# Attention into the first 512 nodes of a graph network computed from a dense count matrix, beside the gathers for the other nodes

## The chip, the cores and the metric

One core of a Trainium2 chip runs the whole program in one launch. The metric is device microseconds (us) of one execution, from the first instruction to the last, as the median of several.

## The reference

A pre-norm graph network of four layers over N = 3125 nodes with D = 128 features and 103125 directed edges (50000 in both directions and one loop per node), sorted by destination. Three layers sum or average neighbours; the fourth, which matters here, is attention along the edges:

```
Q, K, V = x@Wq+bq, x@Wk+bk, x@Wv+bv            # 8 heads of 16 features
score = exp(clip(sum(K[src]*Q[dst], -1) / 4, -5, 5))
wV = segment_sum(V[src] * score, dst);  z = segment_sum(score, dst)
h = layer_norm(x + wV / (z + 0.001), gamma1, beta1)
out = x_in + h + relu(layer_norm(h, gamma2, beta2) @ Wo + bo)
```

## The kernel before

Three parts follow one another. **build_counts** (0 to 338 us) makes from the edge list a dense matrix `counts`: 25 tiles of 128 sources in the partitions, 3136 destinations along a row, bf16; an entry is the number of edges between the two. **dense_layers** (338 to 1125 us) runs seven passes over the 25 node tiles; `z_bank` collects products of `y_parts` (a float32 value as three bf16 parts) with `counts`. Pass 6 also makes queries, keys and values and stores them: `keys_values` (1 KB a node) and `query_parts`. SP issues each tile's loads and stores in program order on its queue (`s_in`, `residual`, `self_term` and so on, function `sync_passes` and its helpers).

**attention** (1125 us to the end) goes by edges. A step is 512 edges, four chunks of 128; six steps are a group, with 34 groups and NS = 202 steps. POOL gathers with four indirect DMAs a step the source rows of `keys_values` into a ring of six steps (L1474). ACT makes the one-hot of each edge's destination (square L1509, relu L1516); PE spreads the queries to the edges by it (L1576, `aq_bank`); DVE multiplies by the gathered keys (`prod`, L1711), makes the one-hot the other way (`pick`, L1714), sums over a head (L1717), multiplies the values of the step before by their weights (`msg`, L1722) and clips the scores (L1727); ACT takes the exponentials (L1534, L1537); PE aggregates a group's six steps into 128 destination rows (`acc_bank`, L1592), two steps behind. Each group then ends with `sum_up` (ACT, L1548), `attended`, `first_norm`, `second_norm`, `result` on DVE, two `rstd` on ACT with a table load ahead of each Ln and Exp (L1525, L1526), a transposition and a projection on PE. All engines run a loop of two groups per turn, written out step by step, with the first group and the last three outside the loop. The order in an engine is that of the code; semaphores alone tie the engines together.

Of the kernel before, what the change touches and what calls it, by code (L numbers as in the profile page):

```python
# [41 lines left out]
NG = -(-E // GE)  # L42
NS = -(-E // (GC * P))
LASTBASE = N - P
QW = 42
# [8 lines left out]
PEELED = 5  # L54
AHEAD = 4
# [94 lines left out]
def over_tiles(chain, step, lag):  # L150


    for dt in range(PEELED):
        before = chain.steps
        step(Num(dt))

    def body(k):
        for j in range(TURN):
            step(Num(PEELED + j, k, TURN))

    chain.loop((NT - PEELED) // TURN, (chain.steps - before) * TURN, body)
    for dt in range(NT, NT + lag):
        step(Num(dt))


def over_tiles_ending(chain, step, lag):


    for dt in range(PEELED):
        before = chain.steps  # L170
        step(Num(dt))

    def body(k):
        for j in range(TURN):
            step(Num(PEELED + j, k, TURN))

    chain.loop((NT - PEELED) // TURN - 1, (chain.steps - before) * TURN, body)
    for dt in range(NT - TURN, NT + lag):
        step(Num(dt))

# [25 lines left out]
def program(nc, t):  # L206
    with ExitStack() as ctx:
# [9 lines left out]
        v.query_parts = dram("query_parts", (NP, YW), BF16)  # L217
        v.rel_rows = dram("group_rel_rows", (NC * P,), BF16)
# [66 lines left out]
def build_counts(nc, t, v, counts):  # L285
# [8 lines left out]
    with ExitStack() as ctx:  # L294
# [39 lines left out]
        base_row = sb("group_first", [1, LEAD + NG + 4], I32)  # L334
        query_row = sb("query_first", [1, QN * (NG + 3)], I32)
        gap = sb("gap", [1, NG])
        gap_flag = sb("gap_flag", [1, 2])
# [20 lines left out]
        def _(sp):  # L358
# [19 lines left out]
            sp.dma_start(v.first_index[:, :], t["src_cols"][:, 0:(GS - 1) * GC]).then_inc(first_in, 16)  # L378
# [63 lines left out]
        def _(dve):  # L442
# [15 lines left out]
            chain.step(nc.vector.tensor_scalar(v.bases[:, :], base_row[:, :], float(LASTBASE), None, ALU.min))  # L458
# [5 lines left out]
            chain.step(nc.vector.tensor_scalar(gap_flag[:, 1:2], v.bases[:, LEAD + NG - 1:LEAD + NG], float(LASTBASE), None, ALU.is_lt))  # L464
            chain.step(nc.vector.tensor_tensor(gap_flag[:, 0:1], gap_flag[:, 0:1], gap_flag[:, 1:2], ALU.max))
            dve.wait_ge(rel_ready, 2)
# [146 lines left out]
def dense_layers(nc, t, v, counts, by_edge=False):  # L613
# [6 lines left out]
    with ExitStack() as ctx:  # L620
# [11 lines left out]
        bq = y3[0][:, 7, 0:2 * D].bitcast(F32)  # L632
        bias = [sb("bias_even", [P, 2 * D]), sb("bias_odd", [P, D])]
# [33 lines left out]
        bias_summed, part_ready, qkv_ready = sem("bias_summed"), sem("part_ready"), sem("qkv_ready")  # L667
        z_ld, z_zeroed = (sems("z_ld"), sem("z_zeroed")) if by_edge else (None, None)
# [21 lines left out]
        def sync_passes(sp, passes):  # L690
# [64 lines left out]

            if by_edge:
                sp.wait_ge(z_zeroed, passes[0] + 1)
# [6 lines left out]
            for p in passes:  # L764
                if p == 6:
                    sp.wait_ge(z_ready, NT * 5)
                    sp.dma_start(wq, t["L3_gnn_Wq"]).then_inc(w_q, 16)
                    sp.dma_start(bq, t["L3_gnn_bq"].partition_broadcast(P)).then_inc(w_q, 16)

# [3 lines left out]
                def step(dt):  # L773
# [11 lines left out]
                    stage(lambda d: store_queries(p, d), dt, PEELED - 1)  # L785

                over_tiles_ending(sp_chain, step, PEELED - 1 if p == 6 else min(LAG[p][3] + 2, PEELED - 1))
            if 6 not in passes:
                return
            for sem_, n in ((s_st, nth(ALL, 6, Num(NT - 1))), (x_st, nth(X_OUT, 6, Num(NT - 1))), (h_st, Num(NT - 1)),  # L790
                            (q_st, Num(NT - 1))):
                for back in range(len(sem_)):
                    (n - back).landed(sp, sem_, held)

        def pool_passes(pool, passes):
# [48 lines left out]

            for p in passes:
                if p:
                    weights_landed(pool, p)
                if p == 2:
# [3 lines left out]
                def step(dt):  # L852
# [5 lines left out]
                    stage(lambda d: sum_norm(p, d), dt, 0)  # L858

                over_tiles(chain, step, LAG[p][3] + 1)  # L860

        def tensor_passes(pe, passes):
# [3 lines left out]
            def transpose(p, dt):  # L866
                n = nth(ALL, p, dt)
                (n + 1).count(pe, h_ready)
                (n - 1).count(pe, hT_ready)
                nc.tensor.transpose(t_bank[n.slot()][:, 0:P], h[:, n.slot(), :], v.ident[:, :]).then_inc(t_done, 1)  # L870

            def products(p, dt):
# [12 lines left out]
                if p == 6:  # L885
                    ins = nc.tensor.matmul(out_[:, 2 * D:3 * D], hT[:, n.slot(), :], wq, start=True, stop=True)
                ins.then_inc(d_done, 1)
# [80 lines left out]
            for p in passes:  # L968
# [20 lines left out]
                over_tiles(chain, step, TURNED[p])  # L989

        def scalar_passes(act, passes):
# [24 lines left out]
            def query_part(p, dt):  # L1016

                if p == 6:
# [3 lines left out]
                    else:  # L1022
                        (dt - 2).landed(act, q_st)
                    nc.scalar.activation(q_part[:, dt.slot(), 0:D], qkv[:, dt.slot(), 2 * D:3 * D], ACT.Copy,
                                         scale=float(DH) ** -0.5).then_inc(part_ready, 1)

# [56 lines left out]
            for p in passes:  # L1083
                def step(dt):
# [12 lines left out]
                    if p == 6:  # L1097
                        stage(lambda d: query_part(p, d), dt, last + 2)
                    if not norm:
                        stage(lambda d: next_h(p, d), dt, norm)  # L1100

                over_tiles(chain, step, LAG[p][3] + 2 * (p == 6))

        def vector_passes(dve, passes):
# [128 lines left out]
            for p in passes:  # L1233
# [22 lines left out]
                over_tiles(chain, step, LAG[p][3] + 1 + 2 * (p == 6))  # L1256
# [18 lines left out]
def attention(nc, t, v, counts):  # L1275
# [7 lines left out]
    QUERIES_AHEAD = 2  # L1283
    QB = 3
    THIRD, THIRD_SHIFT = 171, 9
    MR = 6
    PAIR = 2 * GS
    WIDE = GC * P
    BN, MV, LOG, RSTD = slice(0, 6), slice(6, 8), 8, 9
    with ExitStack() as ctx:  # L1290
# [14 lines left out]
        out_sum, res = room.take("out_sum", [P, D]), room.take("res", [P, 2, D])  # L1305
        src_cols = sb("a_src", [P, NC], I32)
# [18 lines left out]
        q_bank, acc_bank = ps("aq_bank", QB), ps("acc_bank", 2)  # L1325
        (small_bank,), (place_bank,) = ps("at_bank", 1), ps("place_bank", 1)
        t_bank, c_bank = small_bank[:, 0:P], small_bank[:, P:P + D]
        places, upper = place_bank[:, 0:P], place_bank[:, P:P + 1]
        (weight_bank,) = ps("weight_bank", 1)
        weights = weight_bank[:, 0:2 * GC * H].rearrange("p (n c h) -> p n c h", n=2, c=GC)  # L1330
# [13 lines left out]
        held = sem("a_held")  # L1344
        block = ctx.enter_context(nc.Block())
# [12 lines left out]

        def by_power(g):
# [3 lines left out]
        def over_steps(step, chain=None, per_turn=0):  # L1363
# [8 lines left out]
            turns = NG // 2 - 2  # L1372
# [4 lines left out]
        def tail(step):  # L1377
            for i in range(PAIR * (NG // 2 - 1), PAIR * (NG // 2) + GS + 3):
# [3 lines left out]
        def _(sp):  # L1382
            sp.dma_start(src_cols[:, :], t["src_cols"]).then_inc(src_ld, 16)
            sp.dma_start(rel_cols[:, :], v.rel_cols).then_inc(cols_ld, 16)
            sp.dma_start(first_wide[:, :], t["group_first"].partition_broadcast(P)).then_inc(cols_ld, 16)
# [12 lines left out]
            def load_wide(g):  # L1398
# [3 lines left out]
                sp.dma_start(rel_wide[:, g.slot(), :], v.rel_rows[bass.ds(g.value(GE), GE)].partition_broadcast(P)).then_inc(  # L1402
# [10 lines left out]
            def load_h(g, base):  # L1413
                (g - 1).count(sp, h1_ready, held)
                sp.dma_start(h_in[:, g.slot(), :], v.h[bass.ds(base, P), :]).then_inc(h_ld[g.slot()], 16)

            def load_x(g, base):
                (g - 1).count(sp, res_ready, held)
                sp.dma_start(x_in[:, g.slot(), :], v.x[2][bass.ds(base, P), :]).then_inc(x_ld[g.slot()], 16)

            def store(g, base):
                (g + 1).count(sp, res_ready, held)
                sp.wait_ge(out_st, (g + 1).value(16))
                sp.sem_inc(held, 1)
                sp.dma_start(t["out"][bass.ds(base, P), :], res[:, g.slot(), :]).then_inc(out_st, 16)

            def turn(g, both, i):
                regs, query_regs = both
                if group(g + 1):
                    load_wide(g + 1)  # L1430
                    load_queries(g + 1, query_regs[i * QN:i * QN + QN])
                if group(g):
# [11 lines left out]
            load_queries(Num(0), first_bases)  # L1444
            sp.dma_start(wo[:, :], t["L3_gnn_Wo"]).then_inc(w_ld, 16)
# [8 lines left out]
            with sp.Fori(0, NG // 2 - 2) as k:  # L1454
# [3 lines left out]
            for p in range(NG // 2 - 1, NG // 2 + 1):  # L1458
                regs = bases(p)
                for i in range(2):  # L1460
                    turn(Num(2 * p + i), regs, i)
            sp.wait_ge(out_st, NG * 16 + 16)
# [759 lines left out]
```

## Time and profile before

| | us |
|---|---|
| median of three executions | 2166.93 (2166.40 to 2169.04) |
| profiled execution | 2167.79, its span 2166.1 |
| attention, of the span | 1125 to 2166 |
| busy over the span | PE 1557.6, DVE 1399.9, POOL 1173.9, ACT 1094.2 |
| mean granted TensorE clock | 0.696 of full speed |

Busy shares are means over parts with other limits; the attention part is read by itself, from 150 us stretches and from the chain of work that ended last. A full speed of 1.00 of the granted clock is 2.4 GHz, and 0.50 is 1.2 GHz.

### The profile page before, as it was taken

The page shows a single profiled execution, that of the slowest core. Times are in us where ns is not written, and L with a number is a line of the kernel's source. Part 1 is how long each engine was busy: PE and PEld are TensorE (multiplying, and loading weights), DVE is VectorE, ACT ScalarE, POOL GpSimd, SP SyncE. Part 2 cuts the span into 40 slices and gives each one's busy share as a digit, 9 for nine tenths or more (in the row PEclk, how much of TensorE's full clock was granted, in tenths as well). Part 3 has the DMA queues.
Part 4 walks back from the last instruction along what each step waited for, and adds up shares of the span by engine and source line. Part 5 has one row for each costly group of instructions (what it writes and reads, how often), then busy time and mean ns, then how long its engine had stood idle before and what let it go on. Part 6 is the DMA issues. An engine that isn't in the chain of part 4 may idle for free. (4 is left out here: it accounts for less than half of the span.)

```text
span 2166.1 us, 41707 instructions
## 1 busy us (share of the span) xinstructions
PE 1557.6 (72%) x7805; PEld 1038.9 (48%) x7805; DVE 1399.9 (65%) x3771; ACT 1094.2 (51%) x2721; POOL 1173.9 (54%) x1478
## 2 busy tenths in 40 slices
PE   2677776899998999999965556556655566555564
PEld 1232333465555666666644445445444455444453
DVE  7999996545655643335656666666666666666665
ACT  6788885433553422222225555555555555555552
POOL 6645554323543411011127777777777777777774
PEclk9555557999999999999985555555555555555555
DMA  3000001101111110111345444444444444444442
GB/s 149 0 0 0 0 0 49 46 28 44 53 52 53 55 38 29 32 29 58 102 143 157 140 132 142 146 145 144 127 142 145 145 138 133 142 145 144 144 128 63
DMA packets 158830, 192.74 MB, mean 89 GB/s; under 512 B 39725, under 2 KB 126894, under 8 KB 158510
## 3 DMA queue, kind: packets, MB, share of 16 engines
q0 software_dynamic: 38784, 105.96, 16.8%
q1 hardware_dynamic: 119982, 86.09, 12.9%
q8 instruction: 20, 0.33, 0.1%
q14 instruction: 44, 0.36, 0.1%
HBM read 163.23 MB, written 25.04 MB: 87 GB/s over the span
## 5 line engine op out<-in xcount | busy, mean ns | idle before, releaser
L1474 POOL DMA_INDIRECT counts<-keys_values,a_index x788 | 747.0, 948 | 240.1 <-issue 172.5
L895 PE MATMUL z_bank<-y_parts,counts 128*128 128x384 bf16 (+1 forms) x3658 | 641.9, 327 | 1.2 <-DVE y_parts L1231 0.6
L1592 PE MATMUL acc_bank<-counts 128*128 128x136 f32 x1616 | 426.6, 443 | 197.2 <-DVE counts L1722 180.9
L1592 PEld LDWEIGHTS acc_bank<-counts 128*128 128x128 f32 x1616 | 364.8, 321 | 247.5 <-DVE counts L1722 226.0
L895 PEld LDWEIGHTS z_bank<-y_parts,counts 128*128 (+1 forms) x3658 | 358.4, 98 | 228.8 <-issue 5.5
L1711 DVE TENSOR_TENSOR counts<-aq_bank,counts 128x512 f32<-128x512 f32 x202 | 139.6, 691 | 315.0 <-DMA counts<-keys_values,a_index 303.6
L1576 PE MATMUL aq_bank<-counts 126*128 126x128 bf16 x808 | 118.2, 299 | 238.9 <-DVE counts L1711 221.1
L1534 ACT ACTIVATE weight_bank<-a_clipped 128x32 f32<-128x32 f32 x202 | 40.0, 198 | 457.3 <-DVE a_clipped L1727 457.1
L428 POOL TENSOR_TENSOR key_low_build<-iota_b_build,src_cols_build 128x768 bf16<-128x768 bf16 x102 | 155.2, 1522 | 149.8 <-DVE flat_build L506 130.4
L1576 PEld LDWEIGHTS aq_bank<-counts 126*128 126x128 bf16 x808 | 73.7, 129 | 287.0 <-issue 263.1
L1122 DVE TENSOR_REDUCE z_sum<-z_bank 128x128 f32<-128x384 f32 x150 | 83.6, 557 | 165.2 <-PE z_bank L895 160.8
L524 DVE TENSOR_TENSOR counts<-share_build,counts 128x275 f32 x408 | 157.3, 440 | 9.9 <-PE share_build L602 5.8
L602 PE MATMUL share_build<-flat_build,src_tile_build 128*128 128x275 bf16 x408 | 108.3, 422 | 75.4 <-ACT src_tile_build L568 40.6
L1509 ACT ACTIVATE a_apart<-counts,a_query_lane 128x512 bf16<-128x512 bf16 x204 | 144.1, 706 | 12.5 <-DMA counts<-group_rel_rows 12.5
L506 DVE TENSOR_TENSOR flat_build<-iota_wide_build,src_cols_build 128x2200 bf16<-128x2200 bf16 x102 | 144.2, 1415 | 2.4
L1516 ACT ACTIVATE counts<-a_apart,a_one 128x512 bf16<-128x512 bf16 x204 | 144.1, 706 | 0.2
L602 PE MATMUL share_build<-flat_build,left_build 128*128 128x275 bf16 x408 | 108.4, 423 | 42.8 <-ACT left_build L568 39.8
L1722 DVE TENSOR_TENSOR counts<-counts,weight_bank 128x512 f32<-128x512 f32 x202 | 136.7, 677 | 0.8 <-ACT weight_bank L1534 0.8
L1717 DVE TENSOR_REDUCE a_score<-counts 128x32 f32<-128x512 f32 x202 | 137.0, 678 | 0.0
L1714 DVE TENSOR_TENSOR counts<-a_rel,place_bank 128x512 f32<-128x512 f32 x202 | 136.7, 677 | 0.0
L1004 ACT ACTIVATE hT<-t_bank 128x128 f32<-128x128 f32 x175 | 48.5, 277 | 170.8 <-PE t_bank L870 166.1
L884 PE MATMUL d_bank<-weights,hT 128*128 128x256 f32 x350 | 114.4, 409 | 18.1 <-ACT hT L1004 17.8
(183 smaller groups left out, 2132.3 us busy)
## 6 DMA issues: line engine op xcount, KB each, us to landing
counts<-group_rel_rows SPq DMA_DIRECT2D x34, 768.0 KB, 5.3
counts<-keys_values,a_index POOLq DMA_INDIRECT x788, 2.7
self_term<-s_out SPq DMA_DIRECT2D x150, 64.0 KB, 1.6
s_in<-self_term SPq DMA_DIRECT2D x150, 64.0 KB, 1.8
residual<-x_in SPq DMA_DIRECT2D x75, 64.0 KB, 1.6
counts<-counts SPq DMA_DIRECT2D x2, 1792.0 KB, 11.4
counts<-query_parts SPq DMA_DIRECT2D x102, 31.5 KB
x_in<-in_x SPq DMA_DIRECT2D x50, 64.0 KB, 1.8
```

Of the source, the lines that this page charges most:

```text
L428: nc.gpsimd.tensor_tensor(square[:, g.slot(), :, :].rearrange("p (h c) n -> p h c n", h=2)[:, :, 0:BY_POOL, :], place.unsqueeze(1).unsquee ...
L506: nc.vector.tensor_tensor(right[:, g.slot(), :, :, :], iota_wide[:, :, :].unsqueeze(1).to_broadcast([P, 2, KW, 4]), keys.unsqueeze(2).to_b ...
L524: nc.vector.tensor_tensor(window, share[GB * j + i][:, 0:KW].rearrange("p (t w) -> p t w", w=WP), window, ALU.add).then_inc(column_sums, 1)
L602: ins = nc.tensor.matmul(share[j * GB + i][:, 0:KW], left[j][:, i % 2 * GB + c, :], right[:, j, i % 2, :, c], start=c % 2 == 0, stop=c % 2 ...
L895: return nc.tensor.matmul(bank(p, dt)[:, 0:width], counts[:, bass.ds(dt.value(P) + source * NA, P)], y3[(p - 1) % 2][:, source, 0:width], ...
L1474: nc.gpsimd.indirect_dma_start(rows_kv[:, j, c, :], None, v.kv, bass.IndirectOffsetOnAxis(column, 0)).then_inc(gathered[j], 16)
L1509: return chain.start(nc.scalar.activation(apart[:, s.slot(), :], rel_wide[:, g.slot(), j * GC * P:(j + 1) * GC * P], ACT.Square, bias=quer ...
L1516: nc.scalar.activation(node_of_edge[:, g.slot(), j * GC * P:(j + 1) * GC * P], apart[:, s.slot(), :], ACT.Relu, bias=one[:, :], scale=-1.0 ...
L1576: ins = nc.tensor.matmul(q_bank[s.slot(QB)][:, c * P:c * P + P], node_of_edge[0:PARTS * QW, g.slot(), (j * GC + c) * P:(j * GC + c) * P + ...
L1592: ins = nc.tensor.matmul(acc_bank[ga.slot()][:, 0:TW], pick[:, s2.slot(MR), c, :], msg[:, s2.slot(MR), c, :], start=j == 2 and c == 0, sto ...
L1711: nc.vector.tensor_tensor(prod[:, :].rearrange("p (c d) -> p c d", c=GC), q_bank[s.slot(QB)][:, :].rearrange("p (c d) -> p c d", c=GC), ro ...
L1717: nc.vector.tensor_reduce(score[:, s.slot(), :], prod[:, :].rearrange("p (n d) -> p n d", d=DH), AX.X, ALU.add).then_inc(sum_done, 1)
```

## The change

The first 31 steps of the attention (15872 edges, all with a destination below 512) are left out: 171 steps in 29 groups remain, and edge, column and query indices are shifted by `SKIP`. The nodes 0 to 511 (DN = 512, four tiles) get their attention from the dense counts in 200 units, one for each of the 25 source tiles and 8 heads, spread over the six steps of groups 0 to 24 as 2, 2, 1, 1, 1, 1. A unit is: a bf16 score product on PE (three parts of keys by three of queries, stacked along the contraction), `below` (Relu) and `power` (Exp) on ACT, `weighted` on DVE (the larger of the exponential and e^-5, times the counts), and a float32 product with the values on PE, which adds all sources in two `value_bank`s.

```
+HEADS = ((0, 1), (2, 3), (4,), (5,), (6,), (7,))
+def below(s, g, h):
+    (u + 1).count(act, scored)
+    nc.scalar.activation(room_below[:, u.slot(), :], score_bank[:, :], ACT.Relu, bias=five[:, :], scale=-1.0).then_inc(limited, 1)
+def power(s, g, h):
+    (u - (PR - 1)).count(act, valued)
+    nc.scalar.activation(weighted[:, u.slot(PR), :], room_below[:, u.slot(), :], ACT.Exp, bias=five[:, :], scale=-1.0).then_inc(powered, 1)
+def score(g, h):
+    u.count(pe, limited)
+    nc.tensor.matmul(score_bank[:, :], key_stack[:, g.slot(), h, :], query_stack[:, h, :], start=True, stop=True).then_inc(scored, 1)
+def value(g, h):
+    (u + 1).count(pe, weighed)
+    nc.tensor.matmul(value_bank[h // 4][:, :], values[:, g.slot() * 2 + h // 4, h % 4 * P:h % 4 * P + P], weighted[:, u.slot(PR), :], ...)
 # DVE, a step, after the clip
+for gw, h in heads(s1, g, j - 1):
+    (u + 1).count(dve, powered)
+    nc.vector.scalar_tensor_tensor(weighted[:, u.slot(PR), :], weighted[:, u.slot(PR), :], LOWEST, tile_counts[:, gw.slot(), :],
+                                   ALU.max, ALU.mult).then_inc(weighed, 1)
 # PE, a step
 spread(s + QUERIES_AHEAD, ...)
+for _, h in now[0:1]: score(g, h)
+for gv, h in heads(s2, g, j - 2): value(gv, h)
 ... acc_bank products of step s - 2 ...
+for _, h in now[1:2]: score(g, h)
```

To make room in PSUM, `aq_bank` has two buffers, not three (`QUERIES_AHEAD` 1, not 2), `acc_bank` one, not two, and the step weights move into `place_bank`, so that `pick` waits for the weights of the step before:

```
-    QUERIES_AHEAD = 2
-    QB = 3
+    QUERIES_AHEAD = 1
+    QB = 2
+                    s.count(dve, weigh_done)
                     nc.vector.tensor_tensor(pick[:, s.slot(MR), :, :], ...
```

The four dense tiles are finished by the same chain as a group, at steps 155, 157, 161 and 163, between the last groups. DVE takes `result`, `second_norm`, `first_norm`, `attended` after the `weighted` units.

Keys and queries must also stand with features in the partitions. Pass 6 gets one more product per tile, `kT`, and in its first four tiles `qT`, two (four) activations on ACT, three (six) POOL instructions that split them in bf16 parts, and a store; nine tiles stand ahead of its loop, not five:

```
+ins = nc.tensor.matmul(out_[:, 3 * D:4 * D], wk_turned, hT[:, n.slot(), :], start=True, stop=True)
+ins = nc.tensor.matmul(t_bank[n.slot()][:, P:2 * P], wq_turned, hT[:, n.slot(), :], start=True, stop=True)
+sp.dma_start(v.kt[...], kT_part[:, dt.slot(), :, :]).then_inc(kT_st[dt.slot()], 16)
```

The first 512 columns of all count tiles are stored to memory at the start of pass 4 (25 x 128 rows of 1 KB, 3200 KB), and read back by tiles in the attention, with the turned keys and the values, five DMAs a group (`load_tile`); `load_stack` reads the turned queries once, eight DMAs of 128 KB:

```
+if p == 4 and not by_edge:
+    sp.dma_start(v.dense_counts.rearrange("(t p) n -> p t n", p=P), counts[...][:, :, 0:DN]).then_inc(dense_st, 16)
```

On PE the first steps of a loop turn stand as follows before (`aq_bank` is the spread of the queries, `acc_bank` the aggregation, `at_bank` transposition and projection of an earlier group):

```order
L1576 MATMUL aq_bank<-counts 128x128 x4
L102 REGISTER_ALU
L1592 MATMUL acc_bank<-counts 128x136 x4
L102 ISA
L1605 MATMUL at_bank<-ident,counts 128x128
L102 REGISTER_ALU x2
L1576 MATMUL aq_bank<-counts 128x128 x4
L1592 MATMUL acc_bank<-counts 128x136 x4
L102 REGISTER_ALU
L1600 MATMUL acc_bank<-counts 128x136
L1611 MATMUL at_bank<-a_wo,counts 128x128
```

and now, the same place (`score_bank` and `value_bank` are a unit's two products):

```order
L1848 MATMUL aq_bank<-counts 128x128 x4
L1500 ISA
L108 ISA
L1873 MATMUL score_bank<-counts 128x512
L108 REGISTER_ALU
L1861 MATMUL value_bank<-counts 128x512
L108 REGISTER_ALU
L1892 MATMUL acc_bank<-counts 128x136 x4
L108 REGISTER_ALU
L1873 MATMUL score_bank<-counts 128x512
L108 ISA
L1915 MATMUL at_bank<-ident,counts 128x128
```

Between the spread and the aggregation of a step stand a score and a value product, and a second score behind it; the score waits there for ACT's `below` of the unit before.

On SP, from the end of pass 3 to the first loads of pass 4, the issues are now (before, L813 is not there and all else is the same):

```order
L759 DMA residual<-x_in 128x128
L771 DMA self_term<-s_out 128x128 x3
L813 DMA dense_counts<-counts 128x25x512
L731 DMA s_in<-self_term 128x128
L721 DMA weights<-in_L_gnn_W_neigh 128x128
L721 DMA weights<-in_L_gnn_W_self 128x128
L723 DMA bias_odd<-in_L_gnn_b_self 128x128
L731 DMA s_in<-self_term 128x128 x3
```

The store of the counts is queued ahead of the `s_in` loads and the weights of the next pass.

## Rows read from the trace of the kernel before

**Rows 1.** The page's costliest groups: the attention's instructions (count, busy, mean ns, idle)
```profile
L1474 POOL DMA_INDIRECT counts<-keys_values,a_index x788 | 747.0, 948 | 240.1 <-issue 172.5
L1711 DVE TENSOR_TENSOR counts<-aq_bank,counts 128x512 f32<-128x512 f32 x202 | 139.6, 691 | 315.0 <-DMA counts<-keys_values,a_index 303.6
...
L1516 ACT ACTIVATE counts<-a_apart,a_one 128x512 bf16<-128x512 bf16 x204 | 144.1, 706 | 0.2
```
**Rows 2.** Chain that ended last, 1614 to 1634 us (start, us, what)
```profile
1616.62 2.73 DMA counts<-keys_values,a_index
...
1620.38 0.94 POOL counts L1474
...
1621.62 2.70 DMA counts<-keys_values,a_index
```
**Rows 3.** Windows: busy us (instructions) of each engine, granted clock, DMA share, GB/s
```profile
core 0: us, PE busy (x) PEld busy (x) DVE busy (x) ACT busy (x) POOL busy (x), PEclk, DMA share, GB/s
55.00:330.00 275.00, 198.07 (x748) 82.64 (x747) 266.27 (x471) 230.33 (x375) 145.37 (x96) 0.51 0.00 0
...
1905.00:2055.00 150.00, 88.18 (x395) 72.59 (x395) 99.85 (x255) 82.37 (x200) 113.43 (x121) 0.52 0.47 144
1045.00:1100.00 55.00, 55.00 (x344) 36.81 (x343) 36.52 (x125) 12.69 (x35) 8.58 (x22) 1.00 0.33 103
```
**Rows 4.** Timeline of PE in the attention, 1612 to 1624 us (start, us, operation, idle before)
```profile
1612.69 0.60 PE L1576 MATMUL aq_bank<-counts 126*128 126x128 bf16 x4 [0.72 <-DVE counts L1711]
1614.47 2.18 PE L1592 MATMUL acc_bank<-counts 128*128 128x136 f32 x8 [1.18 <-DVE counts L1722]
...
1621.86 0.49 PE L1576 MATMUL aq_bank<-counts 126*128 126x128 bf16 x4
1622.19 1.15 PE L1592 MATMUL acc_bank<-counts 128*128 128x136 f32 x8
```
**Rows 5.** The same view near the end, two steps' aggregation at once
```profile
2144.37 4.01 PE L1592 MATMUL acc_bank<-counts 128*128 128x136 f32 x16 [4.25 <-DVE counts L1722]
```
**Rows 6.** Timeline, a gather that begins while a DVE addition runs
```profile
1301.90 0.29 DVE L1656 TENSOR_TENSOR counts<-counts 128x128 f32<-128x128 f32 x1
1301.95 1.07 POOL L1474 DMA_INDIRECT counts<-keys_values,a_index  x1 [0.30 <-ACT a_index L1501]
```
**Rows 7.** Timeline, 1601 to 1612 us, a second such pair on POOL and DVE
```profile
1602.70 0.29 DVE L1656 TENSOR_TENSOR counts<-counts 128x128 f32<-128x128 f32 x1
1602.82 0.99 POOL L1474 DMA_INDIRECT counts<-keys_values,a_index  x1 [0.30 <-issue]
```
**Rows 8.** Timeline, start of pass 4: a load and its use
```profile
770.20 0.34 SPq L703 DMA_DIRECT2D s_in<-self_term  x1
...
774.97 0.35 DVE L1128 SCALAR_TENSOR_TENSOR layer_out<-z_sum,inv_count,s_in 128x128 f32<-128x128 f32 x1
```
**Rows 9.** The page's DMA issues (count, KB each, median us to landing)
```profile
s_in<-self_term SPq DMA_DIRECT2D x150, 64.0 KB, 1.8
counts<-counts SPq DMA_DIRECT2D x2, 1792.0 KB, 11.4
```
**Rows 10.** Tile view of `first_index`, its 10 KB load issued behind `group_rel_cols` (448 KB)
```profile
L378 SPq DMA_DIRECT2D first_index<-in_src_cols x1: 1792/1792/1792, 20.5 to 20.5; - x1
...
DMA to landing us min/median/max: 2.7/3.7/9.2
```
**Rows 11.** Timeline of PE, pass 6
```profile
1053.56 0.38 PE L886 MATMUL d_bank<-y_parts,hT 128*128 128x128 f32 x2
1053.78 3.09 PE L895 MATMUL z_bank<-y_parts,counts 128*128 128x384 bf16 x18
```
**Rows 12.** Timeline of ACT, start of the attention
```profile
1134.52 0.72 ACT L1509 ACTIVATE a_apart<-counts,a_query_lane 128x512 bf16<-128x512 bf16 x1 [12.51 <-DMA counts<-group_rel_rows]
```
**Rows 13.** Timeline, the end: the last step's first DVE instruction
```profile
2141.84 0.69 DVE L1711 TENSOR_TENSOR counts<-aq_bank,counts 128x512 f32<-128x512 f32 x1 [3.34 <-DMA counts<-keys_values,a_index]
```

More of the change, by code:

```diff
@@ L54 @@
 PEELED = 5
+PEELED_LAST = 9
 AHEAD = 4
@@ L147, in loop, with over_tiles @@
         self.steps = start + per_turn * turns
-def over_tiles(chain, step, lag):
-    for dt in range(PEELED):
+def over_tiles(chain, step, lag, peeled=PEELED):
+    for dt in range(peeled):
         before = chain.steps
@@ L158, in body, with over_tiles_ending @@
         for j in range(TURN):
-            step(Num(PEELED + j, k, TURN))
-    chain.loop((NT - PEELED) // TURN, (chain.steps - before) * TURN, body)
+            step(Num(peeled + j, k, TURN))
+    chain.loop((NT - peeled) // TURN, (chain.steps - before) * TURN, body)
     for dt in range(NT, NT + lag):
         step(Num(dt))
-def over_tiles_ending(chain, step, lag):
-    for dt in range(PEELED):
+def over_tiles_ending(chain, step, lag, peeled=PEELED):
+    for dt in range(peeled):
         before = chain.steps
@@ L1357, in group, with tile, unit, tile_landed @@
             return g.k is not None or 0 <= g.c < NG
+        def tile(g):
+            return g.k is not None or 0 <= g.c < NT
+        def unit(g, h):
+            return Num(g.c * H + h, g.k, 2 * H)
+        def tile_landed(engine, g):
+            turn = (g.c // 2 + 1) * 80
+            engine.wait_ge(tile_ld[g.slot()], turn if g.k is None else g.k * 80 + turn)
+        def heads(s, g, j):
+            if j < 0:
+                g, j = g - 1, j + GS
+            return [(g, h) for h in HEADS[j]] if tile(g) else []
+        starts = sorted([(GS * g + GS + 3 * (g < NG - 1), "group", g) for g in range(NG)] + [(at, "tile", i) for i, at in enumerate(TILE_AT)])
+        place_of = {item[1:]: n for n, item in enumerate(starts)}
+        def nth_out(g):
+            return g if g.k is not None or g.c < NT else Num(place_of["group", g.c])
+        def nth_tile(i):
+            return Num(place_of["tile", i])
+        def tiles_at(s, lag):
+            return [i for i, at in enumerate(TILE_AT) if s.k is None and s.c - at == lag]
+        def tile_bank(i):
+            return value_bank[i // 2][:, i % 2 * 2 * P:i % 2 * 2 * P + 2 * P]
         def by_power(g):
@@ L1424, in store @@
+            def store(o, base):
+                (o + 1).count(sp, res_ready, held)
+                sp.wait_ge(out_st, (o + 1).value(16))
                 sp.sem_inc(held, 1)
[L1425 removed]
+                sp.dma_start(t["out"][bass.ds(base, P), :], res[:, o.slot(), :]).then_inc(out_st, 16)
             def turn(g, both, i):
@@ L1583, in step @@
                 s2 = s - 2
+                now = heads(s, g, j)
+                for _, h in now[0:1]:
+                    score(g, h)
+                for gv, h in heads(s2, g, j - 2):
+                    value(gv, h)
                 if sub(s2):
```

440 lines of the change are left out of this document (346 added, 94 removed).

## The prediction

> **What bounds the kernel now.** I read the page's costliest groups first, then the chain of waits, then the windows, and timelines at the places the change touches. The groups show that POOL's gathers cost 948 ns each and that POOL stood 240.1/788 = 0.305 us before each, almost all of it issue; DVE's `prod` stood 315.0 us, of which 303.6 waited for gathered rows [rows 1]. A step of four gathers is thus 4 x (0.948 + 0.305) = 5.01 us. The chain says the same: it runs from a gather's landing over DVE to the next gather and its landing, and the landings begin 5.00 us apart [rows 2]. So the attention is bound by the rate at which POOL issues gathers, and a group of six steps takes 30.06 us. In it the other engines have room: by the window from 1905 us, PE is busy 88.18/150 x 30.06 = 17.7 us, DVE 20.0, ACT 16.5 [rows 3]. PE does this at a granted clock of 0.52, its lower level of 1.2 GHz; in pass 6 it is busy without a gap at 1.00 [rows 3].
>
> **The change part by part.**
>
> *Steps left out.* 31 x 5.01 = 155.3 us less, as long as POOL stays the bound. All below asks whether it does.
>
> *The units beside the gathers.* Groups 0 to 24 take eight units each. ACT gets two 128x512 activations per unit, 16 x 0.706 = 11.3 us [rows 1], so 27.8 of 30.06. DVE gets one 128x512 operation, 8 x 0.69 = 5.5 us [rows 1], so 25.5 of 30.06. Both fit, ACT with 2.2 us left. The work of PE depends on its clock. Two steps' aggregation took 4.01 us, one 2.18 [rows 4, 5]: a further step costs 1.83 us, a 136-column float32 product 0.458, a 512-column one 0.458 x 512/136 = 1.72. The score has 512 bf16 columns, as many as a step's spread, which took 0.49 to 0.60 [rows 4]. Eight units are 17.7 to 18.6 us at the lower level. Six aggregations overlap with what follows by 2.18 - 1.83 = 0.35 each, so the old 17.7 is 15.6 start to start, and the sum 33.3 to 34.2: more than 30.06. At the upper level an aggregation took 1.15, not 2.18 [rows 4], and the sum is 17.6 to 18.0. That aggregation at the upper level came after 6 us in which PE was nearly never idle. I therefore expect that a group that runs over at 1.2 GHz leaves PE without gaps, that its clock rises, and that the six steps of gathers in the ring cover the lag: cost 0, bounds 0 and 25 x 4.1 = 103 us (rival A).
>
> *Waits added.* `pick` waits for the weights of the step before; behind it on DVE stand the sum, `msg`, the clip and the units. The weights are ACT's third instruction of a step that began with that clip, and DVE waits 303.6/202 = 1.5 us a step for rows in any case [rows 1]: 0. With one `acc_bank` the first aggregation of a group waits for `sum_up`, now first in ACT's step; the spread of the next step is queued behind it: below 1 us a group, and covered like the rest: 0. Each score waits for `below` of the unit before; the second score of a step stands behind a value product and an aggregation, over 1.8 us, in which ACT is long done (otherwise rival B).
>
> *Gathers that start under a `weighted`.* `weighted` reads two SBUF tiles. In the trace a gather is longer when a DVE addition of two SBUF tiles is in flight at its start: with 0.24 us of the addition left it took 1.07, with 0.17 left 0.99 [rows 6, 7], against the mean of 0.948: the length grows by what is left beyond some 0.12 us. With `msg` or `prod`, which read PSUM, I saw no such growth. If gathers start at any moment of the 1.25 us, a 0.65 us operation adds (0.65 - 0.12)^2/(2 x 1.25) = 0.11 us, and 200 add 22. The same formula for the 0.29 us operations, seven a group in 34 groups, gives 2.8 us; the excess over the mean that the lengthened gathers (28 of 783 in the loop) have together is about 1.9. So 22 x 1.9/2.8 = 15; I take +14, bounds 0 and 35 (0.65^2/(2 x 1.25) x 200, without the 0.12).
> The Trainium skill speaks against the change here: "SBUF — State Buffer", section "SBUF: two separate sides", says that GpSimd and a DVE operation with two SBUF inputs take one port pair in turn, each for its whole instruction. The rows agree only in part, as DVE's additions kept their 0.29 us under a gather in flight. By the rule every unit could push a gather by its full length; that is rival P.
>
> *Pass 4.* The store of 3200 KB (3.28 MB) now stands ahead of the `s_in` load that was issued at 770.20 and used at 774.97 [rows 8]. In pass 6 the DMA engines moved 103 GB/s at a share of 0.33 [rows 3], so at most 312 GB/s, and the store takes at least 10.5 us; 1792 KB took 11.4 to land [rows 9], which would make 20. A 10 KB load behind one of 448 KB took 9.2 us to land [rows 10], so loads wait for what is queued ahead. Issue at 770.2, 10.5 for the store and 1.8 for the load [rows 9] give 782.5, less 774.97: 7.5 late, and some 1.5 at a lower clock after the gap. +9, bounds 0 (the load is not held up) and 17.
> The Trainium skill, "DMA: Bandwidth & Descriptors", section "Two DMAs through the same engine are not ordered", lets the descriptors of one queue start in order and overlap; by that the load would come somewhat under the full 10.5 us later, which stays inside these bounds.
>
> *Pass 6.* PE is busy all the time, and a 128x128 float32 product holds up the next by 0.22 us [rows 11]: 29 x 0.22 = +6.4, at most 29 x 0.38 = 11 by its busy time. ACT and POOL are busy 23% and 16% of the window there [rows 3], so their parts hide, but for the last tile, whose split and store end the pass: +1.5 (0 to 4).
>
> *Start of the attention.* 13 DMAs now stand ahead of the second group's destinations (768 KB, on SP's queue); ACT waited 12.51 us for the first ones [rows 12], and these do not move. Then ACT has six steps' one-hots to make, before it needs the second. The 1.5 MB take about 5 us at 312 GB/s, partly hidden: +3 (0 to 7).
>
> *End.* Behind the last gather all is done as before [rows 13]; four more tile finishes stand among the last groups, with eight `rstd` of some 3 us that ACT has time for, since no units are left after step 150. +2 (0 to 9).
>
> Sum: 2167.8 (the profiled execution) - 155.3 + 14 + 9 + 6.4 + 1.5 + 3 + 2 = 2048.4. The median of the runs is 0.9 below the profiled execution: 2047.5, so **2047**.
>
> **Rivals.**
> *A. PE stays at 1.2 GHz and is the bound.* For it: in build_counts PE was busy 198/275 = 72% of the time at 0.51 [rows 3], so much work alone does not raise the clock. Against it: nothing there is without gaps for long, and here the overrun itself closes the gaps. At the lower level in all 25 groups: 25 x (33.3 - 30.06) = 81, to 2128, with the larger score 2150; in half of them 2088.
> *P. The port holds in full.* Each of 200 units delays POOL by its 0.65 us: 130 in place of 14, 2163, no change that could be told. Against it: a growth of at most 0.12 us is what the trace shows.
> *B. Slower: exposed turns on PE's queue.* Place: the score that waits for `below` with values, aggregation and spread queued behind it. If ACT, at 27.8 of 30.06, is late, each such wait shows a score and an activation, 0.5 + 0.7 = 1.2 us. At the lower clock two such waits a group would make 33.3 + 2.4 = 35.7, beyond the 34.9 (30.06 + 120/25) from which the change loses. With four in eight it is 38.1: 2047 + 25 x 8.0 = 2247. For it: all engines are in order and hang on each other within a step. Against: a stalled PE lags, and the ring of six steps and ACT's table of one-hots a group ahead give it slack.
> *That the change does not do what it says:* the edge path by DMA accumulation is taken if edge 15871 ends at node 512 or above; with 33 edges a node it ends near 481. Left out.
>
> **How the numbers follow.** Forecast 0.72; its own range, from the bounds of the port (0 to 35), pass 4 (0 to 17), the other edges and a part of the low clock, is 2024 to 2076. Better than 2024: 0.05. A 0.13, half of it under 2108. P 0.04, B 0.06. So 2024 to 2108 holds about 8 in 10. About 0.2%, some 4 us, is what a measurement here tells from no change; only P falls near it. Faster 0.91, same 0.02, slower 0.07.
>
> **What would show it.** POOL's gathers still 1.25 us apart through the groups with units, with `prod` waiting for the rows; mean gather 0.95 to 1.05 us; PE's granted clock in these groups above 0.52 and near 0.5 after step 150; ACT near 27.8 us a group. At the start of pass 4, a stall of 5 to 12 us behind the store; pass 6 longer by 6 to 11. The prediction is wrong if a group takes over 31.5 us, with POOL waiting for a free slot in the ring (DVE or PE late), or if gathers average over 1.1 us.

## The result, and the profile after

The changed kernel takes 2057.89 us, median of four executions (2054.04 to 2060.99), against 2167.0: a ratio of 0.9494 (95% interval 0.9475 to 0.9513). It is faster by 109 us where 120 were forecast. Its profiled execution took 2059.49 us, with a span of 2057.3. Where the difference lies between the two profiled executions:

| stretch | before | after | change | forecast |
|---|---|---|---|---|
| start to first gather | 1125.93 | 1145.81 | +19.9 | 9 + 6.4 + 1.5 = +16.9 |
| first gather to last | 1011.7 | 878.5 | -133.2 | -155.3 + 14 + 3 = -138.3 |
| last gather to the end | 28.5 | 33.1 | +4.6 | +2 |

The page's groups show that the bound is the same one as in [rows 1]: POOL's gathers, still some 0.31 us apart, with DVE's `prod` waiting for what they fetch. The mean gather went from 948 to 974 ns. PE stood 212.4/200 = 1.06 us for `below` ahead of each score.

```profile
L1695 POOL DMA_INDIRECT counts<-keys_values,a_index x664 | 646.4, 974 | 207.4 <-issue 168.6
...
L1873 PE MATMUL score_bank<-counts 128*128 128x512 bf16 x200 | 85.4, 427 | 221.4 <-ACT counts L1748 212.4
...
L2031 DVE TENSOR_TENSOR counts<-aq_bank,counts 128x512 f32<-128x512 f32 x171 | 118.1, 690 | 139.4 <-DMA counts<-keys_values,a_index 124.7
...
L1755 ACT ACTIVATE counts<-counts,a_five 128x512 f32<-128x512 f32 x200 | 142.4, 712 | 2.4
```

The windows (columns as in [rows 3]) of the groups with units and of those behind them: the granted clock is 0.88 where the units are, with PE busy 68% of the time, and 0.64 after them. Before, it was 0.52 with PE busy 59%.

```profile
1175.00:1925.00 750.00, 513.37 (x2530) 346.96 (x2531) 605.32 (x1433) 636.66 (x1372) 570.30 (x585) 0.88 0.52 151
1925.00:2020.00 95.00, 56.65 (x285) 48.23 (x283) 80.52 (x243) 80.53 (x173) 72.15 (x76) 0.64 0.47 137
```

PE's timeline in a group with units shows both levels. A score takes 0.39 us and a value product 0.86 (start to the next start) at the upper one, 0.61 and 1.70 at the lower one. It fell after two waits of 2.08 and 2.46 us in a row, and was back after the 3.4 us of unbroken work from 1615.14 to 1618.52.

```profile
1608.05 0.39 PE L1873 MATMUL score_bank<-counts 128*128 128x512 bf16 x1 [1.70 <-ACT counts L1748]
1608.27 1.02 PE L1861 MATMUL value_bank<-counts 128*128 128x512 f32 x2
1609.13 1.09 PE L1892 MATMUL acc_bank<-counts 128*128 128x136 f32 x8
1612.31 0.38 PE L1848 MATMUL aq_bank<-counts 126*128 126x128 bf16 x4 [2.08 <-DVE counts L2031]
1615.14 0.61 PE L1873 MATMUL score_bank<-counts 128*128 128x512 bf16 x1 [2.46 <-ACT counts L1748]
1615.55 1.91 PE L1861 MATMUL value_bank<-counts 128*128 128x512 f32 x2
1617.25 1.43 PE L1892 MATMUL acc_bank<-counts 128*128 128x136 f32 x8
1618.52 0.39 PE L1848 MATMUL aq_bank<-counts 126*128 126x128 bf16 x4
```

The start of pass 4, which answers to [rows 8]: behind the store, the `s_in` load is issued at 767.84 and used at 779.00, after a wait of 6.90 us; PE stood 6.0 us and ran at the lower clock for some 4 us (granted 0.50 from 780 to 784 us).

```profile
767.23 0.43 SPq L813 DMA_DIRECT2D dense_counts<-counts  x1
767.84 5.13 SPq L731 DMA_DIRECT2D s_in<-self_term  x1
...
779.00 0.35 DVE L1239 SCALAR_TENSOR_TENSOR layer_out<-z_sum,inv_count,s_in 128x128 f32<-128x128 f32 x1 [6.90 <-DMA s_in<-self_term]
...
779.81 0.48 PE L949 MATMUL t_bank<-ident,h 128*128 128x128 f32 x1 [6.01 <-ACT h L1164]
```

At the start of the attention one wait was handed on through three engines: ACT waits 9.97 us for the second group's destinations, queued on SP behind the tile and the turned queries; the weights of step 0 stand behind it on ACT; DVE's `pick` waits for them (the wait that the change adds); and POOL gets no free slot for 5.30 us.

```profile
1170.36 0.72 ACT L1730 ACTIVATE a_apart<-counts,a_query_lane 128x512 bf16<-128x512 bf16 x1 [9.97 <-DMA counts<-group_rel_rows]
...
1170.99 0.18 ACT L1778 ACTIVATE place_bank<-a_clipped 128x32 f32<-128x32 f32 x1
...
1171.20 0.69 DVE L2035 TENSOR_TENSOR counts<-a_rel,place_bank 128x512 f32<-128x512 f32 x1 [5.98 <-ACT place_bank L1778]
...
1176.67 0.94 POOL L1695 DMA_INDIRECT counts<-keys_values,a_index  x1 [5.30 <-DVE counts L2031]
```

Gathers that start under a `weighted`, as in [rows 6, 7]: the pair of units below began at 1478.78, its second operation about 0.60 later; the gather began 0.07 us into that and took 1.44.

```profile
1478.78 1.28 DVE L2053 SCALAR_TENSOR_TENSOR counts<-counts 128x512 f32<-128x512 f32 x2
...
1479.45 1.44 POOL L1695 DMA_INDIRECT counts<-keys_values,a_index  x1 [0.30 <-ACT a_index L1722]
```

### The profile page after: what moved, and what is told of

It is laid out like the page before. It is cut to its first block and busy times, and to the rows that moved or that the text cites. A ratio compares the mean times of both kernels' runs of the same rounds, so it can differ in the third digit from the quotient of the medians.

```text
span 2057.3 us, 42761 instructions
## 1 busy us (share of the span) xinstructions
PE 1559.0 (76%) x8084; PEld 965.3 (47%) x8084; DVE 1440.0 (70%) x3795; ACT 1293.3 (63%) x3022; POOL 1113.4 (54%) x1442
## 5 line engine op out<-in xcount | busy, mean ns | idle before, releaser
L1695 POOL DMA_INDIRECT counts<-keys_values,a_index x664 | 646.4, 974 | 207.4 <-issue 168.6
L1892 PEld LDWEIGHTS acc_bank<-counts 128*128 128x128 f32 x1368 | 233.0, 236 | 113.0 <-issue 91.7
L1873 PE MATMUL score_bank<-counts 128*128 128x512 bf16 x200 | 85.4, 427 | 221.4 <-ACT counts L1748 212.4
L1892 PE MATMUL acc_bank<-counts 128*128 128x136 f32 x1368 | 237.7, 328 | 18.7 <-ACT counts L1767 12.4
L1861 PE MATMUL value_bank<-counts 128*128 128x512 f32 x400 | 228.8, 678 | 2.3 <-DVE counts L2053 2.3
L2031 DVE TENSOR_TENSOR counts<-aq_bank,counts 128x512 f32<-128x512 f32 x171 | 118.1, 690 | 139.4 <-DMA counts<-keys_values,a_index 124.7
L540 DVE TENSOR_TENSOR counts<-share_build,counts 128x275 f32 x408 | 155.3, 439 | 7.9 <-PE share_build L618 5.8
L1755 ACT ACTIVATE counts<-counts,a_five 128x512 f32<-128x512 f32 x200 | 142.4, 712 | 2.4
L1873 PEld LDWEIGHTS score_bank<-counts 128*128 128x128 bf16 x200 | 19.9, 100 | 252.3 <-ACT counts L1748 241.1
L1748 ACT ACTIVATE counts<-score_bank,a_five 128x512 f32<-128x512 f32 x200 | 133.8, 669 | 1.8 <-PE score_bank L1873 1.8
L2053 DVE SCALAR_TENSOR_TENSOR counts<-counts 128x512 f32<-128x512 f32 x200 | 133.5, 686 | 1.7 <-ACT counts L1755 1.6
L1099 ACT ACTIVATE y_parts<-d_bank 128x128 f32 (+1 forms) x150 | 41.2, 274 | 145.5 <-PE d_bank L963 145.4
```

Source lines behind the costliest of these rows:

```text
L540: nc.vector.tensor_tensor(window, share[GB * j + i][:, 0:KW].rearrange("p (t w) -> p t w", w=WP), window, ALU.add).then_inc(column_sums, 1)
L1695: nc.gpsimd.indirect_dma_start(rows_kv[:, j, c, :], None, v.kv, bass.IndirectOffsetOnAxis(column, 0)).then_inc(gathered[j], 16)
L1748: nc.scalar.activation(room_below[:, u.slot(), :], score_bank[:, :], ACT.Relu, bias=five[:, :], scale=-1.0).then_inc(limited, 1)
L1755: nc.scalar.activation(weighted[:, u.slot(PR), :], room_below[:, u.slot(), :], ACT.Exp, bias=five[:, :], scale=-1.0).then_inc(powered, 1)
L1861: nc.tensor.matmul(value_bank[h // 4][:, :], values[:, g.slot() * 2 + h // 4, h % 4 * P:h % 4 * P + P], weighted[:, u.slot(PR), :], start= ...
L1892: ins = nc.tensor.matmul(acc_bank[:, 0:TW], pick[:, s2.slot(MR), c, :], msg[:, s2.slot(MR), c, :], start=j == 2 and c == 0, stop=False)
```

## The experiments

**One SBUF input.** What do the collisions cost?

```
-nc.vector.scalar_tensor_tensor(weighted[...], weighted[...], LOWEST, tile_counts[...], ALU.max, ALU.mult)
+nc.vector.tensor_reduce(weighted[...], weighted[...].rearrange("p (n d) -> p n d", d=1), AX.X, ALU.max)
```

> The changed kernel with `weighted` as a reduction over groups of one element, 128x512, which reads one SBUF tile, in place of the operation on two; the lower bound and the counts are left out of it. Theory: gathers are lengthened by a DVE operation with two SBUF inputs that is in flight at their start, as far as it lasts more than 0.12 us beyond it. In the changed kernel the mean gather is 974 ns and the lengthening over 0.948 is 17.6 us from the second group on; here the mean is 946 to 950 ns and the time 2040 us (2036 to 2044), 17 less. Rival: any 0.69 us DVE operation at a gather's start delays it, or the gathers are longer because of the added DMAs: mean stays near 974 and the time near 2058. Second rival: other waits take the room over, mean 948 but the time above 2050.

Measured: 2039.43 us (2036.56 to 2041.92), ratio 0.9412 (0.9397 to 0.9428); mean gather 947 ns. POOL's row:

```profile
L1695 POOL DMA_INDIRECT counts<-keys_values,a_index x664 | 628.9, 947 | 207.9 <-issue 168.5
```

The lengthening is gone and with it 18.5 us, as the theory said; the added DMAs have no part in it, as they are all still there. DVE did as many instructions of the same size (0.68 us each, 0.69 in the changed kernel). The edit changes the kind of operation as well, so that by itself it doesn't show that the second SBUF input counts. The changed kernel's trace does: 318 of its 664 gathers began under one of DVE's other four operations of that length (`prod`, `pick`, the sum and `msg`, each with one SBUF input), and none of them took over 0.96 us; 100 began under a `weighted`, and took up to 1.44.

**Half a value product.** Does the clock follow the sum of PE's work?

```
+wide = DN if g.k is None else DN // 2
-nc.tensor.matmul(value_bank[h // 4][:, :], ..., weighted[:, u.slot(PR), :], ...)
+nc.tensor.matmul(value_bank[h // 4][:, 0:wide], ..., weighted[:, u.slot(PR), 0:wide], ...)
```

> The changed kernel with the value product over 256 of the 512 columns in the 22 groups of the loop; half of the sums are left out there. Theory of the prediction: TensorE's clock is up (0.88 from 1175 to 1925 us) because at 1.2 GHz a group would run over 30 us, so that the gaps close. With half the columns a group needs 15.6 + 8 x (0.86 + 0.5) = 26.5 us at 1.2 GHz, which fits: the granted clock of the groups falls to 0.50 to 0.65 and the time stays within 6 us of 2058, as POOL is the bound. Rival: it is the order of the instructions, with a score and a value product between spread and aggregation, that leaves no long gap, whatever the sum: the clock stays over 0.80, the time the same. Rival: PE is on the path in the changed kernel: the time falls by 10 us or more.

Measured: 2058.0 us (2053.86 to 2063.04), ratio 0.9506 (0.949 to 0.9522): no change. The clock fell, but only to 0.77; of the 182 scores in the trace from 1200 to 1900 us, 80 ran at the lower level, against 28 of 181 in the changed kernel.

```profile
1175.00:1925.00 750.00, 482.62 (x2545) 389.75 (x2543) 605.32 (x1437) 635.07 (x1371) 571.28 (x587) 0.77 0.52 151
```

Both theories missed the level. The direction is that of the prediction (less work, longer gaps, a lower clock), but that the work would fit at 1.2 GHz does not send the clock there for good. PE was busy 64% of the time here at 0.77, and 72% in build_counts at 0.51 [rows 3]: the busy share does not tell the level. The time, the same within the spread of the executions, says that PE's work is not on the path.

**The value product twice.** The other side of the same question.

```
+nc.tensor.matmul(value_bank[h // 4][:, :], ..., stop=False)
 nc.tensor.matmul(value_bank[h // 4][:, :], ..., start=False, ...)
```

> The changed kernel with each unit's value product issued twice (the sums of values and weights are doubled by it). Theory: PE is not on the path, because its clock rises with fewer gaps: at the upper level a group takes 17.8 + 8 x 0.86 = 24.7 us of 30.9. The granted clock of the groups rises to 0.95 or more, and the time stays within 5 us of 2058. Rival: PE in its order is near the bound already, its wait for `below` and DVE's wait for the spread lengthen: 2068 or more. In the theory of a fixed lower clock (rival A of the prediction) a group would take 33.3 + 13.8 = 47 us, and the time 2450.

Measured: 2058.9 us (2056.82 to 2063.07), ratio 0.9507 (0.9492 to 0.9521), clock 0.96:

```profile
1175.00:1925.00 750.00, 618.08 (x2878) 385.47 (x2926) 603.89 (x1430) 635.05 (x1366) 571.80 (x585) 0.96 0.52 151
```

As the theory said: 105 us more of PE's busy time in this stretch cost nothing that these runs could tell. The clock rose, and what was idle took it. This is what the step on PE in the prediction rested on.

**`below` twice.** How far is ACT from the path?

```
+nc.scalar.activation(again[:, :], score_bank[:, :], ACT.Relu, bias=five[:, :], scale=-1.0)
 nc.scalar.activation(room_below[:, u.slot(), :], score_bank[:, :], ACT.Relu, ...).then_inc(limited, 1)
```

> The changed kernel with each `below` done twice on ACT, the first into a tile that nobody reads. Theory: ACT is the next bound. It is busy 636.7/750 x 30.9 = 26.2 us a group, and 8 x 0.67 = 5.4 make 31.6, over the 30.9 that the gathers take: at least 0.7 us in each of 25 groups, 2076, and up to 2110 if its waits for scores and for the clip don't overlap. POOL then waits for slots or indices. Rival: the waits in ACT's order take more than its work, so that the slack is gone long before: 2110 to 2200. Rival: nothing, within 5 us of 2058.

Measured: 2063.25 us (2058.11 to 2064.96), ratio 0.9515 (0.9501 to 0.953). That overlaps the changed kernel's interval; all three expectations are off, the last by the least. In the changed kernel ACT stood 106.0 us for the clip from 1175 to 1925 us, here 4.3, and DVE now waits 54.5 us for `power` (the waits of ACT in the first, of ACT and DVE in the second):

```profile
ACT place_bank L1778 <- DVE a_clipped L2048: 106.0, 93, 3.0
```
```profile
ACT place_bank L1780 <- DVE a_clipped L2050: 4.3, 8, 1.4
...
DVE counts L2055 <- ACT counts L1757: 54.5, 46, 1.9
```

So ACT's slack is used up and no more. The expectation priced a `below` at its busy time of 0.67; but the second one started 0.57 us after the first in all 181 pairs from 1200 to 1900 us, so that eight more cost 4.6 us a group, against the 106/750 x 30.9 = 4.4 us that ACT had been idle. In the profiled execution POOL's gap at the start is 7.84 us, not 5.30, and the gathers are lengthened by 22.8 us, not 17.9 (what is over 0.948, from the 21st on); the first gather came 2.1 us earlier.

**The store in pieces.**

```
-sp.dma_start(v.dense_counts.rearrange(...), counts[...][:, :, 0:DN]).then_inc(dense_st, 16)   # once, ahead of pass 4
+sp.dma_start(rows(v.dense_counts, dt), counts[:, bass.ds(dt.value(NA), DN)]).then_inc(dense_st, 16)   # each tile of pass 4
...
```

> The changed kernel with the store of the dense counts cut in 25 stores of 128 KB, one in each tile's step of pass 4, behind that tile's loads. Theory: the one store of 3200 KB held up the loads queued behind it (DVE waited 6.90 us for `s_in`), and cost 8.7 us with the slower clock behind it; in pieces of some 0.4 us it costs nothing, as pass 4 uses 0.13 of the DMA engines: no wait for `s_in` over 1 us at the start of pass 4, time 2049 (2045 to 2053). Rival: PE's pass is as long with the pieces, because each piece holds up a load: 2055 or more.

Measured: 2047.72 us (2046.55 to 2051.39), ratio 0.9449 (0.9433 to 0.9465), 10.2 less than the changed kernel. DVE waits for no `s_in` from 765 to 800 us any more, and the first gather starts at 1136.58. As the theory said: the store's place, not its bytes, had the price. The trace gives that price more exactly than two medians can, of which each is known to some 3 us. From the first tile's sum (`z_sum`) in pass 4 to that in pass 5 it took 113.61 us before the change, 122.27 with the one store and 113.61 with the pieces (before, after and this run):

```profile
771.99 0.56 DVE L1122 TENSOR_REDUCE z_sum<-z_bank 128x128 f32<-128x384 f32 x1 [1.67 <-PE z_bank L895]
...
885.60 0.56 DVE L1122 TENSOR_REDUCE z_sum<-z_bank 128x128 f32<-128x384 f32 x1 [2.32 <-PE z_bank L895]
```
```profile
769.15 0.56 DVE L1233 TENSOR_REDUCE z_sum<-z_bank 128x128 f32<-128x384 f32 x1 [1.67 <-PE z_bank L982]
...
891.42 0.56 DVE L1233 TENSOR_REDUCE z_sum<-z_bank 128x128 f32<-128x384 f32 x1 [2.32 <-PE z_bank L982]
```
```profile
768.26 0.56 DVE L1231 TENSOR_REDUCE z_sum<-z_bank 128x128 f32<-128x384 f32 x1 [1.66 <-PE z_bank L980]
...
881.87 0.56 DVE L1231 TENSOR_REDUCE z_sum<-z_bank 128x128 f32<-128x384 f32 x1 [2.32 <-PE z_bank L980]
```

**The destinations first.**

```
 load_tile(Num(0))
+regs = bases(0)
+load_wide(Num(1))
+load_queries(Num(1), regs[1][0:QN])
 load_stack()
...
```

> The changed kernel with the loads of the second group's destinations and queries issued ahead of `load_stack`, the small weights and the tile of group 1. Theory: in the changed kernel ACT waited 9.97 us for these destinations, DVE's `pick` waited behind it for the weights (5.98 us) and POOL stood 5.3 us for a free slot. Here the destinations land before ACT has made the first six one-hots: POOL's gap goes, time 2053 (2050 to 2056). Rival: the first score waits for the turned queries longer, the spread of step 2 stands behind it on PE, and POOL's gap stays: 2057 to 2062.

Measured: 2057.03 us (2055.15 to 2060.57), ratio 0.9499 (0.9483 to 0.9515): no change that could be told. In the trace POOL's gap is half as long, 2.71 us, and has another cause: the weights of step 0 are ready at 1160.56, but now the first score waits for the turned queries, and ACT stands 6.74 us for it.

```profile
1167.09 0.61 PE L1877 MATMUL score_bank<-counts 128*128 128x512 bf16 x1 [11.84 <-DMA counts<-query_parts_turned]
1167.73 0.69 ACT L1752 ACTIVATE counts<-score_bank,a_five 128x512 f32<-128x512 f32 x1 [6.74 <-PE score_bank L1877]
...
1173.11 0.94 POOL L1699 DMA_INDIRECT counts<-keys_values,a_index  x1 [2.71 <-DVE counts L2035]
```

Theory and rival each hold for half: of what is queued on SP there, something always comes last.

**`weighted` in two halves.**

```
+for half in (slice(0, DN // 2), slice(DN // 2, DN)):
+    ins = nc.vector.scalar_tensor_tensor(weighted[:, u.slot(PR), half], weighted[:, u.slot(PR), half], LOWEST, tile_counts[:, gw.slot(), half], ALU.max, ALU.mult)
...
```

> The changed kernel with each `weighted` as two operations of 128x256 in place of one of 128x512. Theory: a gather that starts while such an operation runs waits for the rest of it beyond 0.12 us, and no longer, so shorter operations hold it up less. A 128x256 one should take about 0.42 us (between 0.29 for 128x128 and 0.69): 400 x (0.42 - 0.12)^2 against 200 x (0.69 - 0.12)^2 is 0.56, and of the 17.6 us of lengthening some 10 stay: mean gather about 962 ns, time 2050 (2046 to 2054). DVE gets 8 x 0.15 = 1.2 us a group more and stays below 27 of 30.9. Rival: the gather waits for both halves, as they follow each other at once: mean 974 to 980, time 2058 to 2062.

Measured: 2055.88 us (2050.25 to 2060.09), ratio 0.9495 (0.948 to 0.9509): no clear gain, between the ranges of theory and rival, and so is the mean gather of 968 ns. Under one unit (two halves in 0.76 us) the law held: each gather waited for the end of the half it had met, by 0.25 us at most, and the lengthening there fell from 7.8 to 4.3 us. Under two units in a row it rose from 9.3 to 10.1: of these gathers seven missed the ends between the operations and waited 0.6 to 1.2 us. One of them:

```profile
1313.85 1.42 DVE L2054 SCALAR_TENSOR_TENSOR counts<-counts 128x256 f32<-128x256 f32 x4
1313.95 2.14 POOL L1695 DMA_INDIRECT counts<-keys_values,a_index  x1 [0.30 <-issue]
```

**All three, and the units apart.**

> The changed kernel with the store of the counts in 25 pieces (2047.7 alone), the loads of the second group's destinations ahead of the turned queries (2057.0 alone) and `weighted` in two halves. If the three places are independent, the gains add: 10.2 + 0.9 + 7.7 = 18.8, time 2039 (2035 to 2044). Rival: what one saves another wait takes, since POOL's ring is then filled by other things: 2045 or more.

Measured: 2043.96 us (2040.94 to 2044.93), ratio 0.943 (0.9417 to 0.9443). The three measured gains (10.2, 0.9 and 2.0) make 13.1, and 13.9 came, so nothing speaks against independent places; but two of the three gains are below what their runs can tell from nothing, and a finer proof this is not. The expectation is 5 us off because the halves had been priced at 7.7.

```
+units = heads(s1, g, j - 1)
+if len(units) == 2:
+    weigh_unit(*units.pop(0))       # ahead of msg; the other one stays behind the clip
```

> The version with all three edits, with the first unit of the steps that have two moved ahead of `msg` on DVE, so that never more than one unit's two halves run in a row. In the version with halves, gathers that started under one unit's halves were lengthened by at most 0.25 us, but under two units in a row some waited 0.6 to 1.2 us: they missed each gap between the operations. Lengthening there: 10.8 us in the 48 rows of two units, 4.6 in the 104 single ones. Theory: a unit by itself costs 4.6/104 = 0.044 us, 200 cost 9 us in place of 15.4, mean gather 960 ns, none above 1.25 us, time 2038 (2034 to 2042). Rival: `msg` comes 0.75 us later in these steps and DVE waits for ACT's `power`, which takes the gain: 2044 or more.

Measured: 2042.63 us (2040.34 to 2046.07), ratio 0.9419 (0.9407 to 0.9432), the fastest whole kernel of the study. No gather is longer than 1.23 us, so the long waits went with the two units in a row (in the version with all three, eight of the nine gathers that waited 0.6 us or more began under two units); but the lengthening is 14.4 us, not 9, since units that stand apart meet more gathers. It cannot be told from the version with all three.

## Why the prediction was right

The forecast was 10.9 us low. The places and waits came as the prediction has them, but for the reason given for PE's clock; several terms were too small, and a gain that nobody forecast hides part of it. Pass 6 cost 4.3 us more than forecast, the collisions some 3.3, the end 2.6, the start 2.0 and the way to the first gather 1.8, while pass 4 cost 0.3 less and the passes ahead of it came out 2.8 us faster in this execution.

- **POOL stays the bound.** Right: from 1175 to 1925 us POOL waited 0.30 to 0.31 us before each gather, as before, and the only longer wait is the one at the start. 31 steps went at the price that the chain gave.
- **The clock of PE**, the step on which most hung. Right in the time (cost 0) and in the direction; the half and the double value product show that PE's work, from 483 to 618 us in 750, changes the clock from 0.77 to 0.96 and not the time. Rival A did not come: from the second group on, the granted clock of each whole group with units was 0.83 to 1.00. Why the level is held so well with gaps of 1 to 2 us in each step is not settled; the prediction's reason, that an overrun closes the gaps, gives the half product a lower clock than it has. So the cost of 0 is shown, and the reason given for it is not.
- **The collisions**: +14 forecast, with bounds of 0 and 35; 17 to 18.5 measured (the page's mean over 664 gathers, and the run without them). The law itself, the rest of the operation beyond 0.12 us, held gather by gather: with 0.61 us left 1.44 (the fence above), with 0.30 left 1.12:

```profile
1315.23 0.68 DVE L2053 SCALAR_TENSOR_TENSOR counts<-counts 128x512 f32<-128x512 f32 x1
...
1315.61 1.12 POOL L1695 DMA_INDIRECT counts<-keys_values,a_index  x1 [0.30 <-issue]
```

  The term was too small because the scaling by 1.9/2.8 took off too much: unscaled it was 22, and a factor of some 0.8 would have fitted. Rival P's price, the full 0.65 us for each unit, did not come. Its rule in the Trainium skill ("SBUF — State Buffer", section "SBUF: two separate sides"), that whoever starts first has the ports for its whole instruction, agrees with the trace in this direction up to the 0.12 us, as a gather that starts second waits for the rest of DVE's instruction. It does not hold here in the other: the pair in the fence above began 0.10 us after the clip before it, like any instruction, with a gather in flight from 1478.19 to 1479.14, and 162 of the 200 units began with a gather in flight and took 0.68 to 0.72 us like the rest.
- **Pass 4**: +9 forecast, 8.7 measured by the sums shown with the store in pieces, and 7.6 to 8.7 in the six other versions with the one store. One bound of the working was wrong: the DMA engines moved 348 GB/s from 770 to 775 us, more than the prediction's "at most 312".
- **Pass 6**: +7.9 forecast, 12.2 measured from the first tile's sum to the attention's first load (1002.61 to 1125.09 before, 1008.45 to 1143.17 after), and 11.1 to 12.3 in the nine other versions, so the term was too small, not this execution late. From the first to the last tile's sum it is 8.3: the product's 0.22 us is there row for row, 6.4 as forecast, and PE waits 1.6 us in two places. Behind the last sum it is 3.9, where 1.5 was forecast: PE waits 1.0 us longer, and from its last product to the attention's first load, while the last tile's parts are split and stored, it takes 7.0 us in place of 4.6.
- **Up to the first gather.** From the attention's first load to the first gather it took 2.6 us, 0.8 before; the prediction has no term for that, and its cause stays open. All that stands ahead of the first sum of pass 4, which the change all but leaves alone, was 2.8 us faster here, and 2.4 to 6.0 in the nine other versions, than in the one trace of the kernel before. So that the front of +19.9 comes close to the forecast +16.9 is in part luck: -2.8, +8.7, +12.2 and +1.8.
- **The start**: +3 forecast, 5.0 measured, from a wait that the prediction had seen (`pick` behind the weights) and put at 0 since in the steady state DVE waits for rows anyway. At the start it did not hold, as ACT itself was held up by a DMA.
- **The end**: +2 forecast, +4.6 measured; 3.1 of it lie behind the issue of the last store (2047.80 to 2057.3, before 2159.72 to 2166.1), in which no engine is busy; all versions have 9.1 to 9.7 us there. The trace shows what the end waits for: POOL's sequencer stands in its last DRAIN from 2043.31 to 2052.84, 9.53 us, while SP has been done since 2049.53, and the last instructions of all engines follow POOL's next one at 2052.88. Before, that DRAIN took 3.98 us and was over ahead of SP. All ten versions have the 9.53; why it is longer stays open.
- **Rival B.** Its waits came, 1.06 us ahead of each score, eight in a group and not four; at the upper clock a group of 18 us with 8.5 us of waits still fits in 30.9, so its place was right and its lower clock wrong. ACT was not late: it had 4.4 us of slack, twice what the prediction's sum of busy times left, in part because activations in a row overlap (0.57 us apart with `below` twice, each 0.67 long).

## What to carry to other kernels

Work put beside a bound by issue is free only where it doesn't touch the issuer: here PE's and ACT's additions beside the gathers were, and the one DVE operation with two SBUF inputs, which lengthens POOL's gathers, cost some 18 us; look at the lengths of the bound engine's own instructions by what was in flight at their start. A large store that nobody waits for still delays the loads queued behind it, so cut it and spread it over a stretch with idle DMA engines. Slack is read from idle time with its releaser, not from a sum of instruction lengths, which overlap.

## What the runs showed of the hardware

In these runs a GpSimd indirect DMA that started while a VectorE operation with two SBUF inputs ran was longer by the rest of that operation less 0.12 us; under one with one SBUF input it was not longer at all (none of 318 over 0.96 us). The other way round nothing was held up: 162 of 200 such VectorE operations began with a gather in flight and took 0.68 to 0.72 us like the rest. Between operations that follow each other at once the gather mostly gets its turn, but seven gathers of the run with halves waited through the next ones too, up to 1.20 us. POOL's DRAIN at the end of the program took 9.53 us in all ten versions and 3.98 before. TensorE's granted clock was 0.52 with the engine busy 59% of the time, 0.51 with 72%, 0.77 with 64%, 0.88 with 68% and 0.96 with 82%: the share alone does not order them.
